# Decoder layer on one core: W, QX and PO as plain fp32 products instead of three fp32r products each

## What is computed

```python
# self attention: 16 heads of 64, 4 key/value heads, rotary, ALiBi
q = (x @ Wq).reshape(b, l, H, HD).transpose(0, 2, 1, 3)
k = (x @ Wk).reshape(b, l, KV, HD).transpose(0, 2, 1, 3)
v = (x @ Wv).reshape(b, l, KV, HD).transpose(0, 2, 1, 3)
...
attn = jax.nn.softmax(attn, axis=-1)
out = jnp.einsum('bhqk,bhkd->bhqd', attn, v)
out = out.transpose(0, 2, 1, 3).reshape(b, l, H * HD)
return out @ Wo                                    # W in the kernel
...
# cross attention to ctx, 16 heads of 16, windows of 64 tokens
qh = split_heads(_proj(q, ln_q_w, ln_q_b, w_q, b_q))   # QX in the kernel
kh = split_heads(_proj(k, ln_k_w, ln_k_b, w_k, b_k))
vh = split_heads(_proj(v, ln_v_w, ln_v_b, w_v, b_v))
...
return _proj(o, ln_o_w, ln_o_b, w_o, b_o)              # PO in the kernel
...
# feed forward with ternary weights and inputs of 8 bits
gate = jax.nn.silu(_bitlinear(x, w_gate))
up = _bitlinear(x, w_up)
return _bitlinear(gate * up, w_down)
...
x = _layernorm(x + _L0_attn_ref(x, ...), axis=-1)
x = _layernorm(x + _L0_xattn_ref(x, ctx_1024, ctx_1024, ...), axis=-1)
x = _layernorm(x + _L0_ffn_ref(x, ...), axis=-1)
```

## Time and profile before

| | us |
|---|---|
| median of 3 runs | 2222.89 |
| lowest and highest | 2222.48, 2224.62 |
| profiled execution | 2226.64 |
| its span, first to last instruction | 2224.7 |
| busy: PE, PEld | 2139.7, 1665.7 |
| busy: DVE, ACT, POOL | 1906.7, 1699.2, 1420.7 |

### The profile page before, as it was taken

How to read it: one execution, slowest core, us unless ns; L and a number is a source line. 1 busy time by engine, 2 the same in 40 slices (tenths; PEclk the granted TensorE clock), 3 DMA queues, 4 the chain that set the end, 5 groups by cost and what they waited for, 6 DMA issues and landing times. The chain is left out here.

```text
span 2224.7 us, 58431 instructions
## 1 busy us (share of the span) xinstructions
PE 2139.7 (96%) x19659; PEld 1665.7 (75%) x19722; DVE 1906.7 (86%) x7884; ACT 1699.2 (76%) x4746; POOL 1420.7 (64%) x1670
## 2 busy tenths in 40 slices
PE   7899999999999999999999999999999999999986
PEld 6677777777777777777777777777777777777764
DVE  5778888888988889988888898888988888889876
ACT  4687778887778887777888777888777788877752
POOL 2566666666766666776666676666677666667531
PEclk9999999999999999999999999999999999999999
DMA  4010101101110110110110111011011111011100
GB/s 165 11 35 25 37 25 35 27 25 37 37 36 24 28 37 26 37 37 25 35 28 25 37 37 34 26 28 37 26 37 37 25 35 28 25 37 37 27 21 11
DMA packets 85399, 74.68 MB, mean 34 GB/s; under 512 B 18544, under 2 KB 79344, under 8 KB 85104
## 3 DMA queue, kind: packets, MB, share of 16 engines
q1 hardware_dynamic: 85104, 70.93, 11.8%
HBM read 45.72 MB, written 8.39 MB: 24 GB/s over the span
## 5 line engine op out<-in xcount | busy, mean ns | idle before, releaser
L1464 POOL TENSOR_TENSOR prob<-prob,precs 128x512 f32<-128x512 f32 x512 | 528.5, 1040 | 551.3 <-DVE precs L1053 548.0
L1372 ACT ACTIVATE prob<-prob,nmax 128x256 f32<-128x256 f32 x1024 | 508.6, 504 | 46.0 <-DVE nmax L1046 46.0
L1046 DVE CUSTOM_DVE_ANT_0 prob<-bank,alibi 128x256 f32<-128x256 f32 x1024 | 371.5, 419 | 23.3 <-PE bank L760 23.2
L1379 ACT COPY pT<-bank 128x512 f32<-128x512 f32 x512 | 302.8, 591 | 57.0 <-PE bank L644 55.8
L644 PE MATMUL bank<-ident,prob 128*128 128x128 f32 x2048 | 316.0, 277 | 3.5 <-ACT pT L1379 3.0
L1396 ACT ACTIVATE px<-px,nmx 128x128 f32<-128x128 f32 x1024 | 313.7, 398 | 6.2 <-DVE nmx L1158 6.2
L644 PEld LDWEIGHTS bank<-ident,prob 128*128 128x128 f32 x2048 | 231.1, 141 | 55.5 <-issue 39.2
L779 PE MATMUL bank<-pT,v_sb 128*64 128x256 f32 x2048 | 250.4, 387 | 4.0 <-DVE qq_lo L1037 3.6
L1158 DVE CUSTOM_DVE_ANT_0 px<-bank,mask 128x128 f32<-128x128 f32 x1024 | 226.4, 287 | 3.7 <-issue 1.7
L779 PEld LDWEIGHTS bank<-pT,v_sb 128*64 128x64 f32 x2048 | 137.2, 137 | 101.2 <-issue 39.9
L1460 POOL TENSOR_TENSOR qtok<-qtok,by_sin 128x512 f32<-128x512 f32 x128 | 164.7, 1287 | 56.0 <-DVE by_sin L1027 46.1
(11 more groups left out here) (223 smaller groups left out, 5950.0 us busy)
## 6 DMA issues: line engine op xcount, KB each, us to landing
raw<-in_xT SPq DMA_DIRECT2D x32, 256.0 KB, 3.0
xtok<-in_x SPq DMA_DIRECT2D x32, 256.0 KB, 2.9
kx_tok<-in_ctx SPq DMA_DIRECT2D x32, 256.0 KB, 3.0
raw<-in_ctxT SPq DMA_DIRECT2D x32, 256.0 KB, 3.0
kx<-k_sin SPq DMA_DIRECT2D x256, 32.0 KB, 2.0
vs<-vx SPq DMA_DIRECT2D x64, 128.0 KB, 2.3
out_y<-x SPq DMA_DIRECT2D x31, 256.0 KB, 3.2
cellk<-in_cell SPq DMA_DIRECT2D x32, 64.0 KB, 3.8
```

The lines of the kernel that those rows point to most:

```text
L1046: v.tensor_tensor_reduce(out=prob[:, (2 * p + q) % SLOTS, c, :], in0=psum[SCORES[c]][:, q * L:(q + 1) * L], in1=alibi[:, p % 2, :], scale= ...
L1372: nc.scalar.activation(prob[:, (2 * p + q) % SLOTS, c, :], prob[:, (2 * p + q) % SLOTS, c, :], ACT.Exp, bias=nmax[:, i:i + 1], scale=-1.0, ...
L1379: nc.scalar.copy(pT[:, p % 2, :, :, q * P:(q + 1) * P].rearrange("p c k n -> p (c k) n"), bank[:].rearrange("p (c n) -> p c n", c=4)).then ...
L1464: g.tensor_tensor(prob[:, n % SLOTS, :, :], prob[:, n % SLOTS, :, :], precs[:, 2 * n:2 * n + 2].unsqueeze(2).to_broadcast([P, 2, L]), ALU. ...
```

## The change

The inputs and weights of W, QX and PO are kept once, as fp32, and each chunk is one plain fp32 product instead of three fp32r ones. The subtractions for oT_lo and yT_lo are gone from VectorE with their entries in the three tables (O, NX and NO), as are the splits of wo, wqx and wox at the start; wo is now loaded in place. ScalarE's copies write fp32 and now tell themselves that the input is ready and the bank free. The other entries of all tables stand in the order they had; the rest of the tables' difference is where their lines break.

```diff
     "dve": [
...
-        (3, 'BX', 0), (3, 'BX', 1), (3, 'OS'), (3, 'NO'), (1, 'R', 3), (2, 'O', 3), (1, 'S', 2), (1, 'Q', 1, 2),
+        (3, 'BX', 0), (3, 'BX', 1), (3, 'OS'), (1, 'R', 3), (1, 'S', 2), (1, 'Q', 1, 2), (3, 'PO'), (3, 'FS'),
...
-            (raw_wo, a["wo"].rearrange("(k p) n -> p k n", p=P)),
+            (wo[:], a["wo"].rearrange("(k p) n -> p k n", p=P)),
...
-            def by_token(bank, xs, ws):
-
-                parts = ((xs[0], ws[0]), (xs[1], ws[0]), (xs[0], ws[1]))
+            def by_token(bank, x, w):
+
                 for t in range(TT):
-                    for i in range(KT * 3):
-                        k, (x, w) = i // 3, parts[i % 3]
-                        last = mm(bank[:, t * D:(t + 1) * D], x[:, k, t * P:(t + 1) * P], w[:, k, :], start=i == 0, stop=i == KT * 3 - 1)
+                    for k in range(KT):
+                        last = mm(bank[:, t * D:(t + 1) * D], x[:, k, t * P:(t + 1) * P], w[:, k, :], start=k == 0, stop=k == KT - 1)
                 return last
...
-                        parts = ((oT_hi, wo_hi), (oT_lo, wo_hi), (oT_hi, wo_lo))
-                        for t in range(TT):
-                            for i in range(PAIRS // 2 * 3):
-                                k, (xs, ws) = i // 3, parts[i % 3]
-                                last = mm(psum[bank][:, t * D:(t + 1) * D], xs[:, k, t * P:(t + 1) * P], ws[:, PAIRS // 2 * h + k, :],
-                                          start=i == 0, stop=i == PAIRS // 2 * 3 - 1)
+                        for t in range(TT):
+                            for k in range(PAIRS // 2):
+                                last = mm(psum[bank][:, t * D:(t + 1) * D], oT[:, k, t * P:(t + 1) * P], wo[:, PAIRS // 2 * h + k, :],
+                                          start=k == 0, stop=k == PAIRS // 2 - 1)
...
-                        by_token(psum[bank], (yT_hi, yT_lo), (wqx_hi, wqx_lo)).then_inc(sem["QX_mm"], 1)
+                        by_token(psum[bank], yT, wqx).then_inc(sem["QX_mm"], 1)
...
-                        by_token(psum[bank], (noT_hi, noT_lo), (wox_hi, wox_lo)).then_inc(sem["PO_mm"], 1)
+                        by_token(psum[bank], noT, wox).then_inc(sem["PO_mm"], 1)
...
-                    elif kind == "O":
-                        u, = args
-                        half = slice(2 * (u % 2), 2 * (u % 2) + 2)
-                        dve.wait_ge(*at("oT_hi", b, u))
-                        v.tensor_tensor(oT_lo[:, half, :], bank[:].rearrange("p (m n) -> p m n", m=2), oT_hi[:, half, :].bitcast(F32),
-                                        ALU.subtract).then_inc(sem["oT_ready"], 1)
...
-                    elif kind == "NX":
-                        dve.wait_ge(*at("yT_hi", b))
-                        v.tensor_tensor(yT_lo[:], bank[:].rearrange("p (k n) -> p k n", k=KT), yT_hi[:].bitcast(F32), ALU.subtract)\
-                            .then_inc(sem["yT_ready"], 1)
...
-                        nc.scalar.copy(oT_hi[:, half, :], bank[:].rearrange("p (m n) -> p m n", m=2)).then_inc(sem["oT_hi"], 1)
+                        nc.scalar.copy(oT[:, half, :], bank[:].rearrange("p (m n) -> p m n", m=2)).then_inc(sem["oT_ready"], 1)
...
-                        nc.scalar.copy(yT_hi[:], bank[:].rearrange("p (k n) -> p k n", k=KT)).then_inc(sem["yT_hi"], 1)
+                        nc.scalar.copy(yT[:], bank[:].rearrange("p (k n) -> p k n", k=KT)).then_inc(sem["yT_ready"], 1)
```

More of the change, by code:

```diff
@@ L46 @@
     x_hi=1, x_lo=1, proj_mm=5, V_mm=1, rot_prod=6, rot_sum=5, q_raw=4, q_cos=4, v_ready=1, kT_mm=1, k_hi=1, k_ready=1, qT_mm=4, q_hi=4, q_ready=4,
-    S_mm=8, s_neg=32, p_exp=32, p_recip=16, p_norm=16, T_mm=16, pT_ready=16, O_mm=4, oT_hi=4, oT_ready=4, W_mm=2, y_half=1, y_ready=1,
-    y_st=2, y_mv=2, y_eps=3, y_rstd=1, x1_norm=1, x1_ready=1, NX_mm=1, yT_hi=1, yT_ready=1, QX_mm=1, qx_prod=1, qx_rot=1, QXT_mm=1, qxT_ready=1,
+    S_mm=8, s_neg=32, p_exp=32, p_recip=16, p_norm=16, T_mm=16, pT_ready=16, O_mm=4, oT_ready=4, W_mm=2, y_half=1, y_ready=1,
+    y_st=2, y_mv=2, y_eps=3, y_rstd=1, x1_norm=1, x1_ready=1, NX_mm=1, yT_ready=1, QX_mm=1, qx_prod=1, qx_rot=1, QXT_mm=1, qxT_ready=1,
     c_hi=1, c_lo=1, c_st=2, c_mv=2, c_eps=1, c_rstd=1, KV_mm=2, kx_prod=2, kx_rot=1, vx_ready=2, KXT_mm=1, kxT_ready=1,
@@ L52 @@
     SX_mm=4, sx_neg=32, px_exp=8, TX_mm=8, pTx_ready=8, OX_mm=2, ox_ready=2, BX_mm=2, sx_recip=2, o_ready=2,
-    o_st=2, o_mv=2, o_eps=1, o_rstd=1, NO_mm=1, noT_hi=1, noT_ready=1, PO_mm=1, y2_ready=1,
+    o_st=2, o_mv=2, o_eps=1, o_rstd=1, NO_mm=1, noT_ready=1, PO_mm=1, y2_ready=1,
     f_st=2, f_mv=2, f_eps=1, f_neg=1, f_rstd=1, f_bias=1, x2_ready=1,
@@ L128 @@
         (1, 'load_ctx'), (1, 'load_xtok'), (0, 'load_vs'), (1, 'load_cell'), (2, 'load_cell'), (3, 'load_xT'),
-        (2, 'load_xtok'), (2, 'load_ctxT'), (1, 'load_vs'), (2, 'load_ctx'), (1, 'fill_kx'), (0, 'store'), (4, 'load_xT'),
+        (2, 'load_xtok'), (2, 'load_ctxT'), (1, 'load_vs'), (2, 'load_ctx'), (1, 'fill_kx'), (0, 'store'),
+        (4, 'load_xT'),
     ],
     "pe": [
-        (0, 'fill', 0, 38), (0, 'first', 0), (0, 'first', 1), (0, 'K'), (0, 'fill', 0, 8), (0, 'Q', 0, 1), (0, 'first', 2), (0, 'prep', 1), (0, 'fill', 0, 26), (0, 'prep', 2),
[20 rows of a table removed]
+        (0, 'fill', 0, 38), (0, 'first', 0), (0, 'first', 1), (0, 'K'), (0, 'fill', 0, 8), (0, 'Q', 0, 1),
+        (0, 'first', 2), (0, 'prep', 1), (0, 'fill', 0, 26), (0, 'prep', 2), (0, 'Q', 1, 1), (0, 'fill', 0, 9),
+        (0, 'prep', 3), (0, 'fill', 0, 5), (0, 'qT', 0), (0, 'fill', 0, 24), (0, 'kT'), (0, 'fill', 0, 8),
[22 rows of a table added]
         (1, 'SX', 1), (1, 'TX', 0, 1), (2, 'T', 11), (3, 'qT', 0), (2, 'S', 7), (1, 'SX', 2), (1, 'TX', 1, 0),
@@ L168 @@
         (0, 'first', 0), (0, 'first', 1), (0, 'first', 2), (0, 'prep', 0), (0, 'tables', 0), (0, 'K'), (0, 'Q', 0, 1),
-        (0, 'prep', 1), (0, 'prep', 2), (0, 'prep', 3), (0, 'Q', 1, 1), (0, 'prep', 4), (0, 'tables', 1), (0, 'qT', 0),
[1 row of a table removed]
+        (0, 'prep', 1), (0, 'prep', 2), (0, 'prep', 3), (0, 'Q', 1, 1), (0, 'prep', 4), (0, 'tables', 1),
[1 row of a table added]
         (0, 'qT', 1), (0, 'Q', 0, 2), (0, 'prep', 6), (0, 'Q', 1, 2), (0, 'S', 2), (0, 'prep', 7), (0, 'qT', 2),
[28 rows of a table removed]
[25 rows of a table added]
     ],
@@ L302 @@
         (29, 'SX', 3), (29, 'TX', 3, 0), (30, 'T', 14), (31, 'qT', 1), (29, 'TX', 3, 1), (31, 'S', 0), (29, 'OX', 1),
[11 rows of a table removed]
[12 rows of a table added]
     ],
     "pool": [
[7 rows of a table removed]
[7 rows of a table added]
     ],
 }
-P_WIDE, P_BIAS, P_CENTRED, P_CROSSED, PRE_DVE = 4, 14, 38, 43, 56
+P_WIDE, P_BIAS, P_CENTRED, P_CROSSED, PRE_DVE = 4, 14, 38, 41, 54
 EMPTIED = {
@@ L408, in build @@
         pre_pe = ctx.enter_context(nc.semaphore("pre_pe"))
-        wo_split = ctx.enter_context(nc.semaphore("wo_split"))
         kx_cleared = ctx.enter_context(nc.semaphore("kx_cleared"))
@@ L424, in build @@
         w_lo = sb("w_lo", [P, KT, QKV], F32R)
-        wo_hi = sb("wo_hi", [P, PAIRS, D], F32R)
-        wo_lo = sb("wo_lo", [P, PAIRS, D], F32R)
+        wo = sb("wo", [P, PAIRS, D])
         rope = sb("rope", [P, 2, TT, HD])
@@ L429, in build @@
         q_scale = sb("q_scale", [P, 4])
-        wqx_hi = sb("wqx_hi", [P, KT, D], F32R)
-        wqx_lo = sb("wqx_lo", [P, KT, D], F32R)
+        wqx = sb("wqx", [P, KT, D])
         wkvx_hi = sb("wkvx_hi", [P, KT, 2 * D], F32R)
         wkvx_lo = sb("wkvx_lo", [P, KT, 2 * D], F32R)
-        wox_hi = sb("wox_hi", [P, KT, D], F32R)
-        wox_lo = sb("wox_lo", [P, KT, D], F32R)
+        wox = sb("wox", [P, KT, D])
         ropex = sb("ropex", [P, 2, 2, TT, XD])
@@ L476, in build @@
         pT = sb("pT", [P, 2, 2, TT, L])
-        oT_hi = sb("oT_hi", [P, PAIRS // 2, L], F32R)
-        oT_lo = sb("oT_lo", [P, PAIRS // 2, L], F32R)
+        oT = sb("oT", [P, PAIRS // 2, L])
         y = xtok
         x1 = sb("x1", [P, TT, D])
-        yT_hi = sb("yT_hi", [P, KT, L], F32R)
-        yT_lo = sb("yT_lo", [P, KT, L], F32R)
+        yT = sb("yT", [P, KT, L])
         y_bn, c_bn, o_bn, f_bn, z_bn = [sb(f"{n}_bn", [P, TT, 6]) for n in "ycofz"]
@@ L504, in build @@
         o_tok = qx_tok
-        noT_hi, noT_lo = yT_hi, yT_lo
+        noT = yT
         y2 = x1
@@ L533, in build @@
         raw_ox = stage[0][:, 1536:2048].rearrange("p (k n) -> p k n", k=KT)
-        raw_wo = kx[:].rearrange("p k h n -> p (k h n)").rearrange("p (k n) -> p k n", k=PAIRS)
         tables = [[(rope[:].rearrange("p c t n -> p (c t n)"), a["rope"]), (q_scale[:], a["q_scale"])],
@@ L707, in run @@
                     elif kind == "wo_ready":
-                        pe.wait_ge(wo_split, 2)
+                        pe.wait_ge(later_loaded[1], 16)
                     elif kind == "prep":
@@ L965, in prepare @@
                     dve.wait_ge(crossed_rounded, 3)
-                    for lo, hi, rawer in ((wkvx_lo, wkvx_hi, raw_kvx), (wqx_lo, wqx_hi, raw_qx), (wox_lo, wox_hi, raw_ox)):
```

(25 more changed lines are left out.)

## The result

The changed kernel took 2274.04 us (median of 4 runs, 2273.47 to 2274.68) beside 2223.48 for the kernel before (4 runs, 2222.48 to 2224.62): a ratio of 1.0227, interval 1.0210 to 1.0245, or +50.6 us. The forecast was 2276. The profiled executions took 2226.64 and 2273.74, +47.1; that of before was 3 us above its median, so +47 is all that the two traces can explain.

The account below looks back on a forecast made before the run. TensorE, busy 98.5% of the steady stretch, was taken as the bound. Dearer products +63.5, XQ -7 and tail -3 gave +53.5 us: 2280 us profiled, 2276 us median, with 8 in 10 for 2254 to 2294.

Parts of the forecast that it names:

- Price of a product: W, QX and PO on TensorE: a plain product costs 0.433 us instead of 0.347 or 0.357, +63.5 us for 32 batches.
- Rival B: Plain products on TensorE cost 0.470 us, each stretch opening or closing with an uncovered weight load: 2305 us, chance 0.10.
- Weight loads at nothing: TensorE's weight loads, 72 to 48 a batch, lie beside the passes and were counted as costing nothing.
- Rivals C and D: TensorE: weight loads set the pace, 2124 us, chance 0.03; or fp32 operands are taken in one pass, 2110 us, chance 0.01.
- XQ, -7 us: TensorE's XQ no longer waits for NX's subtraction to free the bank: 0.23 us saved, 31 times.
- The four waits: TensorE's waits at SX2, NX, D0 and TX(1,1), 1.15 us a round, 34 us in 30 rounds, were to stay.
- Rival A: VectorE's relief, 131 us of work and 51 us of waits, dissolves TensorE's four waits: 2242 us, chance 0.13.
- Tail, -3 us: At the end, the NO subtraction leaves the last chain; with its NX neighbour and W's starts, about 3 us saved.

## Why the prediction was right

- **Price of a product.** Forecast was 0.433 us, from the preparation's fp32 products; passes of 0.216 were measured, in W, QX and PO alike, 0.432 a product. A batch was to pay 1.98 us; in the table QX, W0, and PO with W1 pay 0.29, 0.63 and 1.01, together 1.93. Over 32 batches that would be +62 (+63.5 forecast). Rival B's 0.235 a pass was not seen in any of them.
- **Weight loads at nothing.** Right. W's loads are busy 191.77 us in 1024, 0.19 each, beside passes 0.216 apart. By the rule of the Trainium skill weighed in the prediction (page "TensorE: Matmul & The Clock Gate", what overlaps in array packing) W's 16 passes would take some 6.5 us with their loads, an estimate (16 x (0.216 + 0.19)). They took 3.56. The trace decides against the rule for full rows. Rivals C and D fell with the same rows.
- **XQ, -7 us.** This step failed. XQ came 0.12 behind K as foretold, and the gain was gone at T5, the next step, whose bank was freed by ScalarE's copy; the prediction named what releases XQ and did not ask what releases the step behind it. The order of ScalarE's copies holds the 7 us (2267.28 for 2274.04).
- **The four waits stay.** Right: the rest of the round changed by 0.01 us in all, and SX2 starts 0.57 us behind the scores as before; it does so too with the subtractions gone from the kernel before. VectorE's relief became waiting for W's products, 0.6 us at the sum behind W0. Rival A, that it dissolves them, was refuted by adding the subtractions back: the round did not move. VectorE at 1796.1 busy was forecast near 1775; the 110.6 us it lost are less than the 131 of the earlier trace rows and the splits at the start, mostly because an instruction of this size that stands back to back with its neighbour holds VectorE 0.61 us and not its 0.68. The next starts 0.61 later at 182 of the 192 subtractions; for the qx addition, the starts of 1067.93 and 1068.54 shown with QX and PO plain say the same.
- **A fifth wait, missed.** SX0's, 0.20 us a round. It worked for the change, by about the size of the 7 us that failed: QX's 0.29 was partly spent in it. In the regular round the two errors left +1.72, where the forecast had 1.98 - 0.23 = 1.75. The right total is to that extent luck. The recorded working also has a round of 69.2 us, 26 of them in the stretch from 200 to 2000 us; it is 65.7, or 27.4 of them. The sum does not use that figure.
- **The first rounds.** I charged all 32 batches. The first three rounds and the head grew by 2.6 us; at 1.72 a round and with the two W halves that lie ahead of the first NX (1.35) the same charge would be 6.5. The last round grew by 0.5 instead of 1.72. No step of mine held that.
- **Tail, -3 us.** It is -2.7 in the traces; without the subtractions the kernel before has a tail 2.1 shorter, and putting them back in the changed kernel adds 2.5. But with W alone plain and the subtractions kept, the tail was 68.8 as well, 2.5 less than before: so it is open what shortens the tail, and one profile of each kernel is a thin basis.
- **How near the total is.** For the profiled execution the forecast was 2280, and it took 2273.74: +47.1 where +53.5 was forecast, and the first and the last rounds are most of the difference. For the median it was 2276 and 2274.04. That the second is nearer comes from the profiled execution before, 3.2 us above its median.

## What to carry to other kernels

On an engine that is busy without holes, a change of arithmetic was worth the pass spacing times the count, taken from an operation of the same form in the same trace, and little else. For each wait that an edit removes, look one step further on the same engine: which semaphore is second to last there, and what stands queued in front of its producer. Longer work on the bounding engine is partly free up to the next place where it waited for an engine whose chain does not start behind that work; list all such places, also those under 0.2 us.

## What the runs showed of the hardware

- A plain fp32 product with 256 moving columns is two passes at 0.216 us each; an fp32r pass with the same columns is 0.116 in W and 0.119 in QX. Three fp32r passes are cheaper than one plain product by a fifth: 0.35 for 0.43.
- SX0 paid twice for its wait: 0.10 us ahead and 0.12 inside its stretch (SX0 to W0, 1.06 us in every kernel where it waits, 0.94 or 0.95 where it does not). XQ's four starts show nothing of the kind: they span 0.17 us with the wait and 0.18 without.
- ScalarE's copy of 128x512 from a bank took 0.59 us whether it wrote fp32r or fp32.
- A VectorE instruction of 128x512 is recorded at 0.68 us, and the next starts 0.61 us after it; leaving out all 192 subtractions freed 109.7 us of busy time (1905.8 to 1796.1), where count times mean says 131.
